# Finer waits before the Q projection, another order in the last batch and in the last weight splits, scatters four tiles behind their gathers

## The reference

```python
x = x + _L0_conv_ref(_gn(x), ...)          # group norm, then a gate per channel (mean, max, std, median)
t = _to_tokens(x)                          # 8 batches x 256 tokens x 512 channels
t = t + _L1_attn_ref(_ln_t(t), w_q, w_k, w_v, w_o)   # 16 heads of 32, 30*tanh(scores/30), causal
t = t + _L1_ffn_ref(_ln_t(t), ...)         # below
...
scores = softmax(einsum('th,eh->te', xf, gate_w))     # 8 experts
topk_w, topk_i = lax.top_k(scores, 2)                 # two experts a token, weights made to sum to 1
hgated = silu(einsum('th,ehi->eti', xf, wg)) * einsum('th,ehi->eti', xf, wu)
y = einsum('te,eth->th', cw, einsum('eti,eih->eth', hgated, wd))
shared = silu(xf @ sg) * (xf @ su) @ sd
return (y + shared)
```

## Time and profile before

| | |
|---|---|
| median of 3 runs | 744.89 us (743.75 to 745.23) |
| profiled execution, its own time | 744.2 us |
| its span in the profile | 742.5 us |
| mean granted clock of PE | 0.988 of full |
| busy: PE, PEld | 651.2 us (88%), 525.9 us (71%) |
| busy: DVE, ACT, POOL | 392.0 us (53%), 291.1 us (39%), 261.3 us (35%) |
| chain that ended last: PE, DMA, DVE | 56%, 25%, 7% |
| DMA, mean | 84 GB/s |

### The profile page before, as it was taken

How to read it: one execution, slowest core, us unless ns; L and a number is a source line. 1 busy time by engine, 2 the same in 40 slices (tenths; PEclk the granted TensorE clock), 3 DMA queues, 4 the chain that set the end, 5 groups by cost and what they waited for, 6 DMA issues and landing times.

```text
span 742.5 us, 13736 instructions
## 1 busy us (share of the span) xinstructions
PE 651.2 (88%) x5121; PEld 525.9 (71%) x5122; DVE 392.0 (53%) x889; ACT 291.1 (39%) x477; POOL 261.3 (35%) x256
## 2 busy tenths in 40 slices
PE   0215889999999999999699999999799999999991
PEld 0215778888888888887589899998566767667660
DVE  7774264747475747563546994223444443444430
ACT  8651555555555555555343223435112122121110
POOL 1630122222232223221341115857245455454531
PEclk9999999999999999999999999999999999999996
DMA  9600000101010101020315333442665555655542
GB/s 313 254 0 1 1 2 1 59 1 58 0 56 0 56 0 56 0 86 1 143 57 222 120 105 114 145 148 85 241 111 93 107 98 100 112 93 106 102 57 39
DMA packets 24353, 62.08 MB, mean 84 GB/s; under 512 B 3008, under 2 KB 7104, under 8 KB 22912
## 3 DMA queue, kind: packets, MB, share of 16 engines
q1 hardware_dynamic: 14912, 41.16, 15.4%
q0 software_dynamic: 8736, 20.45, 15.3%
q10 hardware_dynamic: 672, 0.03, 0.1%
HBM read 38.56 MB, written 23.07 MB: 83 GB/s over the span
## 4 chain that ended last, share of the span: by engine, by line
PE 56%; DMA 25%; DVE 7%; issue 4%; ACT 1%; POOL 0%; DVEq 0%; POOLq 0%
PE PS L1498 26%; DMA out_tokens<-yo,dest 25%; PE scores L1498 12%; PE scores L1750 5%; PE PS L1609 5%; PE scores L1595 3%; PE PS L1563 1%; PE PS L1552 1%; DVE rden L1172 1%; DVE xt_l L1151 1%; PE PS L1632 1%; DVE bn L1123 1%; DVE wgu_l L1443 1%; DVE T L1205 1%; PE PS L1780 1%
## 5 line engine op out<-in xcount | busy, mean ns | idle before, releaser
L1498 PE MATMUL scores<-xb,sw 128*128 128x256 f32 x768 | 99.1, 286 | 2.5 <-issue 2.5
L1498 PEld LDWEIGHTS scores<-xb,sw 128*128 128x128 f32 x768 | 96.5, 193 | 4.6 <-issue 2.9
L643 POOL DMA_INDIRECT out_tokens<-yo,dest x39 | 61.7, 1583 | 93.3 <-DMA out_tokens<-yo,dest 91.1
L563 POOL TENSOR_SCALAR_AFFINE_SELECT probs<-probs 128x512 f32<-128x512 f32 x64 | 42.8, 692 | 112.0 <-ACT probs L742 112.0
L1498 PE MATMUL PS<-xt_h,w_h 128*128 128x256 f32 x256 | 76.2, 298 | 5.0 <-DVE xt_l L1151 4.1
L891 ACT ACTIVATE es<-scores 128x256 f32<-128x256 f32 x39 | 14.9, 383 | 163.2 <-PE scores L1498 163.2
L1832 PE MATMUL scores<-wd_sb,ehT 128*128 x156 | 73.5, 593 | 1.0 <-DVE ehT L1458 1.0
L1498 PE MATMUL PS<-xt_l,w_h 128*128 128x256 f32 x256 | 73.2, 286 | 0.0
L1498 PE MATMUL PS<-xt_h,w_l 128*128 128x256 f32 x256 | 73.1, 285 | 0.0
L1498 PE MATMUL scores<-wgu_h,xgT_h 128*128 x156 | 65.3, 419 | 4.3 <-DVE xgT_l L1462 4.3
L739 ACT ACTIVATE probs<-scores 128x1536 f32<-128x1536 f32 x32 | 46.6, 1455 | 49.7 <-PE PS L1609 33.2
(11 more groups left out here) (283 smaller groups left out, 1386.5 us busy)
## 6 DMA issues: line engine op xcount, KB each, us to landing
wgu_l<-in_wgu SPq DMA_DIRECT2D x8, 1024.0 KB, 6.7
T<-in_x SPq DMA_DIRECT2D x8, 512.0 KB, 8.0
w_raw<-in_wqkvo SPq DMA_DIRECT2D x8, 512.0 KB, 10.3
x_rows<-x SPq DMA_DIRECT2D x8, 512.0 KB, 2.8
x_cols<-x2T SPq DMA_DIRECT2D x8, 512.0 KB, 2.6
xc<-x_cols SPq DMA_DIRECT2D x8, 512.0 KB, 3.6
out_tokens<-T SPq DMA_DIRECT2D x8, 512.0 KB, 7.4
wd_sb<-in_wd SPq DMA_DIRECT2D x8, 512.0 KB, 6.8
```

The source lines that it names most:

```text
L563: ins = pool.affine_select(out=t, in_=t, compare_op=ALU.is_ge, fill=0.0, base=0, pattern=[[0, HC], [1, P]], channel_multiplier=-1)
L643: pool.indirect_dma_start(out[:, :], bass.IndirectOffsetOnAxis(dest[:, t:t + 1], 0), yo[:, t % 3, :], None, compute_op=ALU.add).then_inc(y ...
L1498: ins = pe.matmul(out, lhs(k, a), rhs(k, b), start=m == 0, stop=m == len(products) - 1)
```

## The change

It has four parts. PE waits for XN0 before the first two channel blocks of Q0 and for XN1 before the other two. In the last batch, the split of `xb` for batch 0 goes from step "last" to step "late", `hidden_chunk(0, 0)` goes directly behind the scores of the last group of heads, `gate_logits` and `gate_top` of batch 6 go back behind `hidden_chunk(0, 1)` and `normalise(7, 3)`, and the shared down matrix is loaded and split earlier; the partial products of "last" get a buffer of their own. The low parts of the weight halves are dealt out anew. A scatter follows its gather by four tiles.

```diff
@@
+        partials = {"mid": rden[:, :], "late": rden[:, :], "last": kf[:, 0:S], "tail": rden[:, :]}
@@
-        DVE_SPLITS = (11, 12, 14, 15)
+        DVE_SPLITS = (12, 13, 14, 15)
@@ SP
             load_tokens(0)
+            sp.wait_ge(tanh_done, 4 * B)
+            sp.dma_start(sw_raw[:, 2, :], ws[:, 2, :]).then_inc(down_loaded, 16)
             store_x2(B - 2)
             store_x2T("last", B - 2, B - 1)
             load_tokens(1)
-            sp.wait_ge(tanh_done, 4 * B)
-            sp.dma_start(sw_raw[:, 2, :], ws[:, 2, :]).then_inc(down_loaded, 16)
@@ POOL, step
                 att_low(b, 2)
+                if not has_front:
+                    down_matrix_low(0)
                 att_low(b, 3)
...
-                    down_matrix_low()
+                    down_matrix_low(1)
@@ POOL
-            low_with_weights(6, (), (0, 1, 2))
-            low_with_weights(7, (8, 9, 10))
-            weight_low(13)
+            low_with_weights(6, (None, None, None, 8), (0, 1, 2))
+            low_with_weights(7, (9, 10, 11))
             for t in range(3, NTILES):
                 gather(t)
-                if t >= 5:
-                    scatter_add(t - 5)
-            for t in range(NTILES - 5, NTILES):
+                if t >= 4:
+                    scatter_add(t - 4)
+            for t in range(NTILES - 4, NTILES):
                 scatter_add(t)
@@ ACT, step
-                else:
-                    split_high(0, 0)
                 att_high(b, 1)
...
-                att_high(b, 3)
                 if not has_front:
                     down_matrix_high()
+                att_high(b, 3)
...
                     values(part, b, 1)
+                    if not has_next:
+                        split_high(0, 0)
                     soft(b + 1, 2)
@@ ACT, gated_shared(b, j, between); between is 14 for the last chunk
                 act.activation(sg[:, j % 2, :], gu_bank[j % 2][:, 0:S], ACT.Silu).then_inc(silu_done, 1)
+                if between is not None:
+                    weight_high(between)
                 act.wait_ge(h_done, CB * b + j + 1)
...
-            weight_high(14)
             weight_high(15)
@@ DVE, step
-                if not has_front:
-                    split_low(0, 0)
...
-                if has_back:
+                if has_back and has_front:
                     gate_top(part, b - 1, b)
                 normalise(b, 3)
+                if not has_front:
+                    gate_top(part, b - 1, b)
...
+                if has_front and not has_next:
+                    split_low(0, 0)
                 add_projection(part, b, 0)
@@ PE
+            def heads_projection(part, item, s, tokens=None):
...
+                    for h in range(2):
+                        if tokens and m == 0:
+                            pe.wait_ge(*emptied(tokens[0], f"XN{h}", tokens[1]))
+                        ins = triple(bank[:, m * S:(m + 1) * S], range(2 * h, 2 * h + 2),
@@ PE, step
                 head_scores(b, 3)
                 if has_front:
-                    if isinstance(b, int) and b == 0:
-                        front_split("ahead", 0)
-                    else:
-                        front_split("mid", b - 1)
-                    heads_projection(part, "Q0", b)
+                    heads_projection(part, "Q0", b, ("ahead", 0) if isinstance(b, int) and b == 0 else ("mid", b - 1))
+                else:
+                    pe.wait_ge(tanh_done, 4 * b + 4)
+                    pe.wait_ge(xb_l_done, 1)
+                    pe.wait_ge(piece_low, 8)
+                    hidden_chunk(0, 0, True, 0)
                 head_values(b, 2)
...
                     hidden_chunk(0, 1, True, 0)
+                    gate_logits(part, b - 1, b)
```

More of the change, by code:

```diff
@@ L264, in layer_kernel @@
         scope.close()
-        partial = rden
+        partials = {"mid": rden[:, :], "late": rden[:, :], "last": kf[:, 0:S], "tail": rden[:, :]}
         def xb_part(parity, part):
@@ L543, in _, with down_matrix_low @@
                                    ALU.subtract).then_inc(wlo_done, 1)
[L545 to L550, removed]
+            def down_matrix_low(h):
+                pool.wait_ge(down_high, h + 1)
+                at_h = slice(1024 * h, 1024 * (h + 1))
+                pool.tensor_tensor(sw_l[:, 2, at_h], sw_raw[:, 2, at_h], sw_h[:, 2, at_h].bitcast(fp32),
+                                   ALU.subtract).then_inc(down_low, 1)
             def rstd_of(var_ready, rstd_ready, b):
@@ L617, in low_with_weights @@
                     hidden_low(b, j)
-                    if j < len(splits):
+                    if j < len(splits) and splits[j] is not None:
                         weight_low(splits[j])
@@ L850, in _ @@
                 for j in range(CB):
-                    gated_shared(b, j)
+                    gated_shared(b, j, 14 if b == B - 1 and j == CB - 1 else None)
                     if j == 1 and b + 1 < B:
@@ L1182, in partial_out @@
                 k, _ = ring(part, "GT", s)
-                dve.tensor_copy(partial[:, :], ring_bank[k][:, 0:S]).then_inc(partial_ready, 1)
+                dve.tensor_copy(partials[part], ring_bank[k][:, 0:S]).then_inc(partial_ready, 1)
             def gate_top(part, b, s):
@@ L1493, in _, with triple @@
         def _(pe):
-            def triple(out, parts, lhs, rhs):
+            def triple(out, parts, lhs, rhs, begins=True, ends=True):
                 products = [(k, a, b) for k in parts for a, b in ((0, 0), (0, 1), (1, 0))]
                 for m, (k, a, b) in enumerate(products):
-                    ins = pe.matmul(out, lhs(k, a), rhs(k, b), start=m == 0, stop=m == len(products) - 1)
+                    ins = pe.matmul(out, lhs(k, a), rhs(k, b), start=begins and m == 0,
+                                    stop=ends and m == len(products) - 1)
                 return ins
@@ L1568, in wslice @@
                 return t[:, j, k * C + lo_:k * C + hi_]
-            def heads_projection(part, item, s):
+            def heads_projection(part, item, s, tokens=None):
                 j = "QK".index(item[0])
@@ L1575, in heads_projection @@
                     lo_ = (2 * int(item[1]) + m) * P
-                    ins = triple(bank[:, m * S:(m + 1) * S], range(CB),
-                                 lambda k, a: wslice((w_h, w_l)[a], j, k, lo_, lo_ + P),
-                                 lambda k, a: (xt_h, xt_l)[a][:, k, :])
+                    for h in range(2):
+                        if tokens and m == 0:
+                            pe.wait_ge(*emptied(tokens[0], f"XN{h}", tokens[1]))
+                        ins = triple(bank[:, m * S:(m + 1) * S], range(2 * h, 2 * h + 2),
+                                     lambda k, a: wslice((w_h, w_l)[a], j, k, lo_, lo_ + P),
+                                     lambda k, a: (xt_h, xt_l)[a][:, k, :], h == 0, h == 1)
                 ins.then_inc(full, 1)
@@ L1640, in gate_logits @@
                 for tt in range(TT):
-                    ins = pe.matmul(ring_bank[k][:, S + tt * E:S + (tt + 1) * E], partial[:, tt * P:(tt + 1) * P],
+                    ins = pe.matmul(ring_bank[k][:, S + tt * E:S + (tt + 1) * E],
+                                    partials[part][:, tt * P:(tt + 1) * P],
                                     fold[:, :], start=True, stop=True)
@@ L1647, in front_transposes @@
                 transposes(part, "XN", front, s)
-            def front_split(part, s):
-                pe.wait_ge(*emptied(part, "XN0", s))
-                pe.wait_ge(*emptied(part, "XN1", s))
             def hidden_chunk(b, j, first, parity):
@@ L1686, in step @@
                     heads_projection(part, "Q1", b)
-                if has_back:
-                    gate_logits(part, b - 1, b)
+                    if has_back:
+                        gate_logits(part, b - 1, b)
                 head_values(b, 3)
@@ L1715, in _ @@
             front_transposes("front", 0, 0)
-            front_split("front", 0)
             pe.wait_ge(wlo_done, 4)
             pe.wait_ge(gate_loaded, 16)
-            heads_projection("front", "Q0", 0)
+            heads_projection("front", "Q0", 0, ("front", 0))
             heads_projection("front", "K0", 0)
```

7 lines of the change are left out of this document (1 added, 6 removed).

## The result

The changed kernel takes 733.7 us (median of 5 runs, 731.3 to 734.48) where the kernel before takes 743.96 (5 runs); the ratio on record is 0.9843, with a 95% interval of 0.9824 to 0.9861. The plain quotient of the two medians, 0.9862, lies just above this interval, so the gain is 10.3 us by the medians and 11.7 by the ratio. Predicted were 734.4 us. The profiled execution has a span of 732.2 us, 10.3 less than before.

A forecast was written before the change was run, and what follows sets the result against it. PE was taken to bound the kernel until the experts, then the chain from scatter to scatter. Terms of -4.0, -5.6, -0.7 and 0 us gave a span of 732.1 and a median of 734.4, range 731.2 to 738.3.

The forecast's parts named there:

- Part 1: Eight Q projections: PE starts on the first half of xt_l, -4.0 us (-2.2 to -4.5).
- a second wait: At each Q projection, the wait for the other half of xt_l would keep some 0.05 us.
- the 0.84 us of slack: Behind a Q projection, att of group 2 was ready 0.84 us before PE came, covering 0.5 of earlier arrival.
- The front's 0.7: At the front's Q projection, the wait shrinks by one half of xt_l and its semaphore, some 0.7 us.
- Part 2: Last batch, last tanh to output projection: earlier hidden chunk at the full clock, -5.6 us (-3.9 to -5.8).
- other end -3.9: Last batch: if the clock falls again, the hidden chunk keeps its 4.53 us and the gain is 3.9.
- One term: Last batch: the first hidden chunk's 4.53 us become 2.83 at the full clock.
- The load of the down matrix: Last batch: load takes 5.7 us, landing at 362.0; rival: 17.8 us, 743 in all, chance 0.02.
- Part 3: Start of the experts: weight halves dealt anew, -0.7 us, half of the clock's 1.5 (+0.9 to -3.2).
- the meetings of DVE and POOL: Weight halves 12 and 13 wait for POOL's 10 and 11; rival without meetings or clock fall: 732, chance 0.14.
- Part 4: Expert tiles: scatters stay 5.12 us apart, 0 (-0.3 to +0.3); rival of late gathers: 748, chance 0.02.
- The sum: Whole kernel: -4.0 - 5.6 - 0.7 + 0, -10.3 to -10.4 us, expected median 734.4.

The follow-up runs named there:

- parts 1, 4 and 2 alone: Three kernels, each the kernel before with only that one part of the change: ratios 0.9931, 1.0007 and 0.9922 in that order.
- part 3 alone: The kernel before with only the weight halves dealt out anew and ACT's high part 14 moved ahead: ratio 0.9999 (0.9981 to 1.0016).
- part 1 alone: The kernel before with only the two separate waits of the Q projection: ratio 0.9931 (0.991 to 0.9953).
- the three without meetings: The changed kernel with no DVE weight half beside a POOL half, 0.9835; also with the hidden chunk put back, 0.9838; also with twelve more matmuls, 0.981.
- The added matmuls: The changed kernel with twelve unneeded matmuls on PE ahead of the last batch's first hidden chunk, 0.9835; also with weight halves dealt without meetings, 0.981.
- scatter three: The changed kernel with a scatter three tiles behind its gather instead of four: ratio 0.9888 (0.9866 to 0.991).

## Why the prediction was right, point by point

**Part 1** (forecast -4.0): right in mechanism. The wait is gone at all seven steps and 0.7 of 1.5 is left in the front. The seven steps gave 4.06 instead of 3.3, 0.58 each: I had left 0.05 a step for a second wait, which isn't there. The rest is in how a wait is read: the idle times of the seven steps are 3.57 in all, but from the start of the last scores matmul to the start of Q0 the seven distances fall from 5.52 to 1.50, by 4.02. Nothing behind it came late: of the 0.84 us of slack that I read from the earlier trace rows 0.22 are left, `att` being done at 208.99 and the values starting at 209.21. The front's 0.7 is there in the wait but not in the sum of two profiles, since the time from the first Q0 to the first values differs by up to 1.9 us between kernels that are alike there (24.73 to 26.61).

**Part 2** (forecast -5.6, other end -3.9): both ends were met, 5.53 where the clock held (13.61, four traces) and 4.04 where it fell (15.10, one trace). Both are within 0.2 of the working. One term was too small: at the full clock the chunk takes 3.14, not 2.83, as the second hidden chunk of the kernel before already shows:

```profile
370.09 3.14 PE L1498 MATMUL scores<-xb,sw 128*128 128x256 f32 x24
```

The hidden chunk's new place, on which the working rests, isn't needed: put back, the chunk is as fast. There the 5.63 us (19.14 to 13.51) are, from start to start, 2.73 up to the chunk (the wait of 2.49 for the split of `xb`, which is made a step earlier), 1.42 of the chunk at the full clock, 1.38 between the partial products and the values of group 3, where the logits and their wait of 0.67 stood, and 0.10 from there to the output projection. The earlier split and the later logits were not run apart. The load of the down matrix came in time: `att_high` of group 3 started 0.04 behind its input (364.13 to 364.17).

**Part 3** (forecast -0.7, from +0.9 to -3.2): the meetings of DVE and POOL came as worked out, at the halves named, and PE began 0.48 earlier instead of at the same time. The size hangs on the clock, as the range said. From the output projection to the first scatter the old deal took 162.28, 162.26, 162.43 and 163.17 us (before, parts 1, 4 and 2 alone), with a clock of 0.50 to 0.70 behind the first matmul every time. The new one took 160.35, 160.44 and 160.46 where it stayed at full throughout, 161.66 where it fell only ahead of the first matmul, and 162.81 and 163.02 where it fell on both sides. By runs, part 3 alone is worth 0.1 us, within 1.4, so its size is not shown. The Trainium skill's rule ("SBUF — State Buffer", section "SBUF: two separate sides"), that of these two engines the one that comes second waits for the other's whole instruction, agrees with the traces: 3.27 and 3.28 us beside a POOL half, 1.21 without one.

**Part 4** (forecast 0): right, 1.0007 alone, within 0.0016.

**The sum** came out within 0.7 us (734.4 against 733.7), and against the first profile it did so by luck, with errors that cancel: part 2 gave 1.6 less there and the front 0.4 less, the seven steps and part 3 together 1.9 more. The runs put it better: parts 1 and 2 alone multiply to 0.9931 x 0.9922 = 0.9854, which is the change's own 0.9843 within the intervals, and parts 3 and 4 add nothing that could be measured.

What stays open is why the clock falls in one execution and not in the next. The wait of 1.60 behind the last scores had a fall behind it in one trace and none in four; the wait of 2.74 had one in part 1 alone and none in the five other kernels that have it, the kernel before among them. But the order of work is not without a part in it. At the first hidden chunk of the last batch the clock was low in all four profiles of the old order (the chunk took 4.46 to 4.60), in one of five of the new order, and in neither of the two with the chunk put back. Behind the first matmul of the experts it was low in all four of the old deal of weight halves, in two of six of the new deal, and in none of the three without meetings. What in the order does this is not shown. The added matmuls removed the wait, but that they keep the clock up is not shown. The Trainium skill, "TensorE: Matmul & The Clock Gate", section "Part 1: The HAM clock gate (the "warmup" mystery)", describes the window in which PE's activity is judged as free-running, not reset by the start of a kernel; by that the same wait may be judged differently each time. That fits these traces, but no run here shows it.

## What to carry to other kernels

Where a consumer waits for the last of several pieces, wait for each piece where it is first used; one and the same wait of some 0.5 us in seven steps added up to 4 us here. Look for a late input before moving the work that waits for it: with the split made a step earlier, the chunk was as fast in its old place as in the new one. Deal work out between VectorE and GpSimd so that their subtractions of two SBUF operands don't lie beside each other, since each meeting of two weight halves cost 2 us on the engine that came second, and then see which load is next in line: here the next wait took more than half of the gain.

## What I had not expected

The granted clock of one and the same program differs from one execution to the next at the same place: 4.63 or 3.14 us for the same 24 matmuls behind the same wait of 1.60, and, in kernels that are alike there, 5.34, 5.85 or 3.98 us from the first matmul of the experts to the first transposes of their products (part 3 alone, scatter three, the changed kernel). These two places alone make some 3 us (1.5 and 1.9), more than parts 3 and 4. One profile of each kernel is then not enough to price a step behind a wait of PE; the same stretch of several kernels that are alike there shows at least how far it varies.
